# Quantised feed-forward stage of a gated decoder: GpSimd, not VectorE, adds the gated second bias to the token tiles

## What is computed

```python
x = x + tanh(g_ffn[0]) * ffn(layernorm(x))
def ffn(t):
    h = layernorm(t) * gamma + beta
    h = quant(h) @ quant(w1).T + b1
    h = gelu(h)
    return quant(h) @ quant(w3).T + b3
```

## Time and profile before

| What | us |
|---|---|
| Median of three runs | 3319.41 |
| The profiled execution, its own time | 3314.45 |
| Its span (first to last instruction) | 3312.5 |
| PE busy in the span | 3114.8 (94%) |
| DVE busy in the span | 1855.0 (56%) |
| ACT busy in the span | 1054.5 (32%) |
| POOL busy in the span | 709.1 (21%) |

### The profile page before, as it was taken

How to read it: one execution, slowest core, us unless ns; L and a number is a source line. 1 busy time by engine, 2 the same in 40 slices (tenths; PEclk the granted TensorE clock), 3 DMA queues, 4 the chain that set the end, 5 groups by cost and what they waited for, 6 DMA issues and landing times. The chain is left out here.

```text
span 3312.5 us, 51997 instructions
## 1 busy us (share of the span) xinstructions
PE 3114.8 (94%) x20493; PEld 2369.8 (72%) x20493; DVE 1855.0 (56%) x2538; ACT 1054.5 (32%) x1555; POOL 709.1 (21%) x589
## 2 busy tenths in 40 slices
PE   7999979988599989999999699999899999999999
PEld 6788855555277775666666578887788888777877
DVE  3111138877788838777777478887566665200000
ACT  2222233322233326445554233333433333200000
POOL 0000020000000013333333245554344443000000
PEclk9999989999799999999999899999999999999999
DMA  5334346775522132222222544444544545643343
GB/s 188 118 114 138 122 143 142 156 168 114 210 74 77 64 119 83 78 95 90 106 85 95 164 151 155 155 155 154 159 154 167 171 161 196 221 156 112 126 144 101
DMA packets 370423, 445.61 MB, mean 135 GB/s; under 512 B 157488, under 2 KB 264624, under 8 KB 367296
## 3 DMA queue, kind: packets, MB, share of 16 engines
q1 hardware_dynamic: 354048, 394.04, 37.8%
q10 hardware_dynamic: 16192, 49.04, 4.0%
HBM read 257.69 MB, written 176.79 MB: 131 GB/s over the span
## 5 line engine op out<-in xcount | busy, mean ns | idle before, releaser
L2753 PE MATMUL g_ps<-g_xs,g_wq 128*128 128x512 f32 x2616 | 633.9, 396 | 0.0
L2753 PEld LDWEIGHTS g_ps<-g_xs,g_wq 128*128 128x128 f32 x2616 | 491.3, 190 | 100.7
L2837 PE MATMUL g_ps<-g_wd,g_h 128*128 128x512 f32 x1536 | 354.2, 391 | 0.0
L2837 PEld LDWEIGHTS g_ps<-g_wd,g_h 128*128 128x128 f32 x1536 | 289.9, 189 | 61.9 <-issue 0.9
L2261 POOL TENSOR_TENSOR g_wq<-g_s,g_wq 128x512 fp32r<-128x512 f32 x168 | 242.3, 1453 | 211.6 <-ACT g_wq L2327 211.6
L2261 POOL TENSOR_TENSOR g_wq<-fe_wt,g_wq 128x512 fp32r<-128x512 f32 x127 | 184.6, 1454 | 249.1 <-ACT g_wq L2323 249.1
L2693 DVE TENSOR_TENSOR g_ta<-g_ps,g_ta 128x1024 f32<-128x1024 f32 x4 | 4.9, 1224 | 374.7 <-PE g_ps L2834 374.7
L1369 PE MATMUL kv_gps<-kv_xh,kv_wh 128*128 128x512 f32 x512 | 205.2, 401 | 1.0 <-DVE kv_xl L1266 1.0
L1369 PE MATMUL kv_gps<-kv_xh,kv_wl 128*128 128x512 f32 x512 | 200.3, 391 | 0.0
L1369 PE MATMUL kv_gps<-kv_xl,kv_wh 128*128 128x512 f32 x512 | 200.2, 391 | 0.0
L1665 ACT COPY a_pt<-a_tps 128x1024 f32<-128x1024 f32 x128 | 129.6, 1013 | 205.7 <-PE a_tps L1821 205.5
(11 more groups left out here) (312 smaller groups left out, 5584.4 us busy)
## 6 DMA issues: line engine op xcount, KB each, us to landing
g_h<-g_hidden SPq DMA_DIRECT2D x176, 256.0 KB, 2.7
g_hidden<-g_h ACTq DMA_DIRECT2D x84, 512.0 KB, 3.6
fe_wt<-g_merged SPq DMA_DIRECT2D x43, 512.0 KB, 4.4
g_merged<-fe_wt SPq DMA_DIRECT2D x41, 512.0 KB, 3.6
kv<-kv_y SPq DMA_DIRECT2D x16, 1024.0 KB, 6.4
early_x<-x SPq DMA_DIRECT2D x32, 512.0 KB, 6.1
g_down<-fe_rows SPq DMA_DIRECT2D x22, 512.0 KB, 6.3
fe_wt<-g_down SPq DMA_DIRECT2D x22, 512.0 KB, 4.0
```

Of the source, the lines that this page charges most:

```text
L2753: w = pe.matmul(ps[:, bank(u, to), :], wq[q % NQ][:, l, P * k:P * k + P], xs[j][:, r, k, :], start=(first and k == 0 and a == 0), stop=(la ...
L2837: w = pe.matmul(to, tile[:, p % RING, l, cols], wd[f][:, r, os], start=(f == 0 and a == 0), stop=False)
```

## The change

`with_bias` moves from VectorE's list to GpSimd's, with the same waits and the same signal. On GpSimd, with_bias(0) and with_bias(1) stand after power(1) behind the wait for `gb`, and with_bias(b+2) behind power(b+2) in each turn. The number of instructions that add is the same, 16, and so are their operands.

```diff
@@ gpsimd
+            def with_bias(n):
+                pool.wait_ge(S["y2"], n + 1)
+                pool.tensor_tensor(x[:, n % 4, :], x[:, n % 4, :], rows[3], ALU.add).then_inc(S["xb"], 1)
+
             power(0)
             power(1)
+            pool.wait_ge(S["gb"], 1)
+            with_bias(0)
+            with_bias(1)
             for b in range(B):
                 if b:
                     power_y(b - 1)
                 if b + 2 < B:
                     power(b + 2)
+                    with_bias(b + 2)
             power_y(B - 1)
@@ vector
-            def with_bias(n):
-                dve.wait_ge(S["y2"], n + 1)
-                dve.tensor_tensor(x[:, n % 4, :], x[:, n % 4, :], rows[3], ALU.add).then_inc(S["xb"], 1)
-
...
                 if b:
                     low(b - 1, 1)
-                else:
-                    dve.wait_ge(S["gb"], 1)
-                    with_bias(0)
-                    with_bias(1)
-                if b + 2 < B:
-                    with_bias(b + 2)
             result(B - 1)
```

## The result

The changed kernel takes 3343.5 us (median of five runs, 3339.2 to 3351.8) against 3319.4 before: the ratio is 1.0072, with a 95% interval of 1.0055 to 1.0089, so it is 24 us slower. The profiled execution has 3343.53 us and a span of 3341.8, 29.3 more than the one before. VectorE is no less busy than before though 16 instructions left it (1875.8 us, 1855.0 before), and GpSimd 746.8 us (709.1).

What follows compares the result with a forecast made beforehand. TensorE was taken to bound the steady tiles, where the move costs and gains nothing; 1.0 us gained at the start of the stage gave 3318.4 us against the median 3319.41. The range was 3312 to 3341 us.

Steps and rivals of the forecast that it cites:

- I take VectorE as the winner: Steady tile: VectorE's L776, starting 0.04 us ahead of GpSimd's add, runs first and the add waits, at no cost.
- the first rival: GpSimd wins at L776, making it 2.27 us late; TensorE loses 1.5 us a steady tile: +21.0, 3340.4 us; chance 0.22.
- 0.08 ahead to 0.04 behind: Earlier trace's L2522 against a GpSimd add: VectorE won starting 0.08 us ahead and lost starting 0.04 us behind.
- in an even contest the first start wins: Argument at L776 that VectorE's 0.04 us lead suffices; with the two-thirds argument it gave VectorE three in four.
- The lock itself: VectorE and GpSimd instructions reading SBUF: one waits for all of the other but some 0.14 us; L776 2.27 us late.
- The slack behind it: Steady tile: TensorE's turn_y(b-1, 1) has 0.83 us of slack after L841, so a late L776 costs 1.5 us.
- wait for `xb` or power_y: A rival: GpSimd's adds come late, so power_y or L827 waits; at most +1.16 us a tile, 3338 us; chance 0.01.
- 3.5 forecast: Steady tile: VectorE's idle gap before L823 grows from 2.60 to about 3.5 us, with no gain in time.
- 1.0 us of gain at the start of the stage: Three adds leave VectorE's list before the first result, so L823 comes at 879.55 instead of 880.50 us.
- such a shift of the clock: Start of the stage: one product may land on another granted clock level, up to 3.2 us either way.
- the likeliest case: VectorE wins at L776; 16 adds removed, 1.0 us kept: 3318.4 us, own range 3312 to 3325, chance 0.74.
- 0.70 more than 1.23 had been reckoned: Start of the stage: VectorE's first L805 meets GpSimd's first add and ends 0.70 us late, at 866.27 instead of 865.57.

Runs made afterwards that it cites:

- second-add: Kernel before, bias add left on VectorE, plus a GpSimd add of the same size on other data in 14 tiles: 3321.0 us, ratio 1.0001.
- two-memset kernels: Changed kernel with two one-column GpSimd memsets between the wait and the add: 3319.8 us, ratio 0.9989 against the kernel before.
- the memset run: Kernel before plus a GpSimd memset of 1024 bf16 columns, reading nothing, at the moment of the moved add, for 14 tiles: 3319.7 us, ratio 0.9995.

## Why the prediction was wrong

**The step that failed** is one sentence: "I take VectorE as the winner." With 0.04 us ahead VectorE lost, in every tile, and the first rival, given a chance of 0.22, is what came. Over all runs GpSimd won each of the 43 meetings at which its add started 0.042 to 0.045 us behind, and lost each of the 27 at 0.11 to 0.12 in the second-add and the two-memset kernels. With the 0.08 of the earlier trace rows, where GpSimd lost, the turn lies between 0.045 and 0.08 us behind, if that one pair of other instructions goes by the same rule. The rows had bounded it rightly (0.08 ahead to 0.04 behind); the error was the argument for a choice inside the bounds, that in an even contest the first start wins. By the profile's starts the contest is not even: GpSimd wins from a little behind.

**Right in the other steps.** The lock itself, from the earlier trace rows: one instruction waits for all of the other but some 0.14 us, which gave 2.27 us for L776, and 2.24 came (0.20 us of overlap for this instruction, and an add of 2.40 us instead of 2.37). The slack behind it: the first rival had 1.5 us for a steady tile and 16.5 for 11 of them; 1.59 and 17.9 were measured. No wait for `xb` or power_y came up. And once GpSimd loses the meeting, the forecast holds: the two-memset kernel takes 0.9989 of the time before, with 3.44 us of idle time ahead of the result of a steady tile (3.5 forecast). Even the 1.0 us of gain at the start of the stage is there: from the first scaling of a product (L802) to the first result lie 16.2 us in its profile and 16.3 to 16.4 in those of the other kernels without a lost early meeting in which GpSimd adds, against 17.5 before. It is too small to show in the times.

**A term mis-sized.** For turns 1 and 2 the rival had 2.27 us each, the bare stall. They cost 3.8 and 4.9, as the second product also ran in part at the lower clock. That is 4.1 us more (8.7 less 2 x 2.27), more than the 2.5 us by which the median lies above even the range, which was drawn up to the rival's 3341. The prediction had named such a shift of the clock, at up to 3.2 us, but for the likeliest case and not for the rival. Ahead of the first result the forecast had 1.0 us of gain, the rival none. Without the 2.7 us that were there before, 1.7 were lost; 0.8 of them lie ahead of L806, where the stage's first product took 6.43 us instead of 5.27, and it waits for no add. The other 0.9 stand behind L806: VectorE's first L809 met the second of GpSimd's two adds, not the first, and took 3.06 us where 0.70 more than 1.23 had been reckoned, and L784 lost its meeting there too.

The Trainium skill (SBUF — State Buffer, "SBUF: two separate sides") says that whichever of the two starts first gets the shared port pair for the whole instruction. That it is for the whole instruction agrees with every meeting here of two instructions that read (L784 ends 1.08 us behind the add that won). That it is the first to start does not, where VectorE leads by 0.045 us or less by the starts that the profile gives. By the same section a GpSimd instruction that only writes doesn't contend with a VectorE one with two SBUF inputs, and the memset run agrees (1.28 us).

## What to carry to other kernels

When work moves from VectorE to GpSimd, look for the VectorE instruction with two SBUF operands that the same semaphore releases: a few hundredths of a us decide which of the two stands still, so don't leave it to them. Let the GpSimd instruction wait for the end of the one that is urgent, and let it meet one with slack. And before pricing freed time on an engine, see what the tile waits for: here 19 us of VectorE's work taken away were worth nothing that the times show, and a change of order in its list, into idle time that was there already, was worth 0.53 us a tile.

## What was not expected of the hardware

GpSimd wins although its instruction starts up to 0.045 us behind VectorE's. Its request may come sooner behind its start than VectorE's does, or the profile may date the starts of the two engines differently; no row shows the request, so this stays open. A second wait ahead of an instruction on GpSimd cost it some 0.065 us (the add starts 0.145 us instead of 0.079 behind the end of the first norm instruction), enough to turn the outcome and 25 us of the kernel.
